# x + ctx of a fused attention and low-rank-expert block made by ScalarE and GpSimd at the head of a pass, the first w in contiguous halves, one wait of the second sample left out

## The reference

```
p = Wp @ layernorm(x);  t = Wt @ ctx;  g = Wg @ ctx
att[group] = sum over the group's 32 rows of p * g
y = Wz(grouped) @ (att * t)
w = x + tanh(g_xattn) * (groupnorm(y) * gn_w + gn_b + ctx)
h = layernorm(w, axis=-1)
gate = softmax over the 16 largest of h @ Wq.T @ keys.T, spread over 64 experts
z = (h @ A.T) * gate (each expert has 8 columns)
out = w + tanh(g_ffn) * 2 * (z @ B.T)
```

## Time and profile before

| what | us |
|---|---|
| median of 3 runs | 340.39 (338.96 to 341.20) |
| the profiled execution's own time | 341.37 |
| its span | 339.6 |
| PE busy | 331.7 (98% of the span) |
| DVE busy | 246.2 (73%) |
| ACT busy | 161.6 (48%) |
| POOL busy | 162.5 (48%) |

### The profile page before, as it was taken

One profiled execution on the slowest core, in us unless ns is written; L12 is line 12 of the kernel. 1 busy time (PEld: TensorE's weight loads), 2 busy tenths in 40 slices (PEclk: granted clock), 3 DMA queues, 4 the chain that ended last, 5 costly groups with the idle time before them and its releaser, 6 DMA issues.

```text
span 339.6 us, 5620 instructions
## 1 busy us (share of the span) xinstructions
PE 331.7 (98%) x2024; PEld 298.8 (88%) x2024; DVE 246.2 (73%) x625; ACT 161.6 (48%) x286; POOL 162.5 (48%) x146
## 2 busy tenths in 40 slices
PE   8999999999999999899999999999999999999996
PEld 6588898899988998788999899898999899989984
DVE  0866996684779879678797697867897785773462
ACT  2596835684374453375516662183535632342310
POOL 0173798199158599055940859036860620010000
PEclk9998999999999999799999999999999999999999
DMA  7999702960912574159521874238621121103002
GB/s 252 409 388 398 279 2 55 353 212 5 322 46 93 182 284 124 31 162 299 194 72 26 245 280 154 62 108 296 234 77 33 32 92 41 54 3 124 2 31 93
DMA packets 21227, 52.21 MB, mean 154 GB/s; under 512 B 2112, under 2 KB 6848, under 8 KB 21200
## 3 DMA queue, kind: packets, MB, share of 16 engines
q1 hardware_dynamic: 20848, 51.65, 44.2%
q10 hardware_dynamic: 352, 0.20, 0.2%
HBM read 41.10 MB, written 10.75 MB: 153 GB/s over the span
## 4 chain that ended last, share of the span: by engine, by line
PE 85%; DVE 8%; POOL 4%; issue 2%; DVEq 0%; POOLq 0%
PE w_ps L1205 16%; PE z_ps L1175 16%; PE w_ps L1091 10%; PE w_ps L1175 9%; PE w_ps L1212 8%; PE z_ps L1042 7%; PE z_ps L1021 4%; PE t_ps L1152 3%; PE w_ps L1069 2%; PE w_ps L1042 2%; PE t_ps L1119 2%; POOL c_lo L365 1%; DVE x_st L706 1%; POOL A_lo L353 1%; PE w_ps L1219 1%
## 5 line engine op out<-in xcount | busy, mean ns | idle before, releaser
L1205 PE MATMUL w_ps<-B_hi,zT_hi 128*128 128x512 f32 x128 | 51.9, 406 | 0.0
L1205 PE MATMUL w_ps<-B_lo,zT_hi 128*128 128x512 f32 x128 | 50.2, 392 | 0.0
L346 POOL TENSOR_TENSOR xT_lo<-xT_in,xT_hi 128x512 fp32r<-128x512 f32 x24 | 35.5, 1498 | 22.0 <-ACT xT_hi L458 19.2
L389 POOL TENSOR_TENSOR y_rs<-y_ve,minus_half 128x2 f32<-128x2 f32 x8 | 5.9, 742 | 71.4 <-DVE y_ve L789 71.4
L365 POOL TENSOR_TENSOR c_lo<-c_sb,c_hi 128x512 fp32r<-128x512 f32 x24 | 30.3, 1303 | 11.7 <-DVE uw L811 11.7
L346 POOL TENSOR_TENSOR cT_lo<-cT_in,cT_hi 128x512 fp32r<-128x512 f32 x24 | 35.5, 1500 | 0.0
L1175 PE MATMUL z_ps<-A_hi,hT_hi 128*128 128x288 f32 x160 | 34.7, 298 | 0.3 <-POOL A_lo L353 0.3
L1212 PE MATMUL w_ps<-B_hi,zT_lo 128*128 128x512 f32 x128 | 34.5, 391 | 0.0
L508 ACT ACTIVATE uw<-w_ps,neg_u 128x512 f32<-128x512 f32 x32 | 20.1, 684 | 30.2 <-DVE neg_u L756 30.2
L1175 PE MATMUL z_ps<-A_lo,hT_hi 128*128 128x288 f32 x160 | 34.1, 295 | 0.0
L525 ACT ACTIVATE hT_hi<-t_ps 128x512 fp32r<-128x512 f32 x32 | 17.5, 595 | 27.9 <-PE t_ps L1152 27.3
(11 more groups left out here) (164 smaller groups left out, 860.7 us busy)
## 6 DMA issues: line engine op xcount, KB each, us to landing
c_sb<-in_ctx SPq DMA_DIRECT2D x16, 512.0 KB, 5.5
x_sb<-in_x SPq DMA_DIRECT2D x16, 512.0 KB, 5.2
xT_in<-in_xT SPq DMA_DIRECT2D x14, 512.0 KB, 7.8
cT_in<-in_cT SPq DMA_DIRECT2D x14, 512.0 KB, 9.1
out_block<-uw SPq DMA_DIRECT2D x14, 512.0 KB, 4.3
z_through<-zg_sb SPq DMA_DIRECT2D x9, 256.0 KB, 2.3
products<-z_through SPq DMA_DIRECT2D x9, 256.0 KB, 2.7
A_in<-in_aT SPq DMA_DIRECT2D x8, 256.0 KB, 12.4
```

Source lines behind the costliest of these rows:

```text
L346: last = pool.tensor_tensor(lo[:, chunks, :], came[:, chunks, :], hi[:, chunks, :].bitcast(f32), ALU.subtract)
L1205: pe.matmul(w_ps[k][:, :], zT_hi[:, t, row], w[:, j, cols], start=(j == 0 and w is B_hi), stop=False)
```

## The change

Four things are edited.

1. From sample 3 on, x + ctx is made by `scale_ctx` on ACT and `x_add` on POOL. `scale_ctx(3)` stands behind `hT_high(1, 2)`, and `scale_ctx(m + 1)` at the end of ACT's pass, behind `hT_high(1, m)`. `x_add(m)` is the first thing in POOL's pass. `x_shift` on POOL and `x_plus_ctx` on DVE are gone from sample 3 on and stay for sample 2. ACT's `exps(0, b)` now stands between the two halves of the transposes' high parts.
2. In DVE's pass `zT_low(0, b)` stands between the two tiles of w, and `minus_means(m + 1)` (which makes beta) behind `zT_low(1, b)`, where it stood ahead of `zT_turn(1, b)`.
3. `first_w(k)` works on contiguous halves of a tile and waits for that quarter's copy of u alone; `hT` of sample 0 waits for `w_done` in both of its groups.
4. `group_means(2)` doesn't wait for `att_rows`.

```
--- before.py
+++ after.py
@@ -374,7 +374,8 @@
 
             def x_add(n):
                 for t in range(T):
-                    pool.wait_ge(c_scaled, per_tile(n, t))
+
+                    pool.wait_ge(c_scaled, per_tile(n if n < 2 else n - 1, t))
                     for cols in pieces():
                         last = pool.tensor_tensor(c_sb[n % 2][:, t, cols], c_sb[n % 2][:, t, cols], x_sb[:, t, cols],
                                                   ALU.add)
@@ -430,8 +431,8 @@
             x_root(3)
             w_root(2)
             c_low(3)
-            x_shift(3)
             for m in range(3, NB):
+                x_add(m)
                 if m + 1 < NB:
                     for h in range(NH):
                         xT_low(h, m + 1)
@@ -443,8 +444,6 @@
                     pool.wait_ge(w_done, per_tile(m, T - 1))
                     c_low(m + 1)
                 w_root(m)
-                if m + 1 < NB:
-                    x_shift(m + 1)
 
         @block.scalar
         def _(act):
@@ -615,11 +614,6 @@
             w_square(1)
             hT_high(1, 1)
             offsets(1)
-            def transposes_high(n):
-                for h in range(NH):
-                    xT_high(h, n)
-                    cT_high(h, n)
-
             for t in range(T):
                 c_high(t, 2)
             residual(1)
@@ -643,11 +637,16 @@
             offsets(2)
             M_high(3)
             hT_high(1, 2)
+            scale_ctx(3)
             for b in range(2, NB - 1):
                 m = b + 1
                 if m + 1 < NB:
-                    transposes_high(m + 1)
+                    xT_high(0, m + 1)
+                    cT_high(0, m + 1)
                 exps(0, b)
+                if m + 1 < NB:
+                    xT_high(1, m + 1)
+                    cT_high(1, m + 1)
                 residual(b)
                 if b < NB - 2:
                     exps(1, b)
@@ -669,6 +668,8 @@
                     M_high(m + 1)
                 hT_high(0, m)
                 hT_high(1, m)
+                if m + 1 < NB:
+                    scale_ctx(m + 1)
             residual(NB - 1)
             exps(0, NB - 1)
             zT_high(0, NB - 1)
@@ -696,7 +697,7 @@
 
                 dve.wait_ge(c_lo_s, from_second(n, T - 1))
                 for t in range(T):
-                    dve.wait_ge(x_shifted, per_tile(n - 2, t))
+                    dve.wait_ge(x_shifted, t + 1)
                     dve.scalar_tensor_tensor(c_sb[n % 2][:, t, :], c_sb[n % 2][:, t, :], tg[:, 0:1], x_sb[:, t, :],
                                              ALU.mult, ALU.add).then_inc(xt_done, 1)
 
@@ -797,15 +798,15 @@
 
             def first_w(k):
 
-                t, g = divmod(k, NH)
-                rows, sums = (parts(a[0][:, t, :])[:, g * KH:(g + 1) * KH, :] for a in (uw, c_sb))
-                dve.wait_ge(u_copied, per_use(0, NH * t + NH - 1))
+                t, cols = use(k)
+                dve.wait_ge(u_copied, per_use(0, k))
                 dve.wait_ge(xt_done, per_tile(0, t))
-                dve.scalar_tensor_tensor(rows, rows, slope[:, t:t + 1], sums, ALU.mult, ALU.add).then_inc(
-                                             w_done if k % NH == NH - 1 else w_half, 1)
-
-            def w_tiles(n):
-                for t in range(T):
+                last = dve.scalar_tensor_tensor(uw[0][:, t, cols], uw[0][:, t, cols], slope[:, t:t + 1],
+                                                c_sb[0][:, t, cols], ALU.mult, ALU.add)
+                last.then_inc(w_done if k % NH == NH - 1 else w_half, 1)
+
+            def w_tiles(n, tiles=range(T)):
+                for t in tiles:
                     dve.wait_ge(u_copied, u_use(n, NH * t + NH - 1))
                     dve.wait_ge(xt_done, per_tile(n, t))
                     dve.scalar_tensor_tensor(uw[n % 2][:, t, :], uw[n % 2][:, t, :], slope[:, t:t + 1],
@@ -963,7 +964,6 @@
             minus_means(3)
             for b in range(2, NB - 1):
                 m = b + 1
-                x_plus_ctx(m)
                 gate(0, b)
                 if b < NB - 2:
                     x_stats(m + 1)
@@ -973,12 +973,13 @@
                 u_statistics(m, (0,))
                 group_deviation(m)
                 slopes(m, lambda: zT_turn(0, b))
-                w_tiles(m)
+                w_tiles(m, (0,))
                 zT_low(0, b)
+                w_tiles(m, (1,))
                 if b < NB - 2:
-                    minus_means(m + 1)
                     zT_turn(1, b)
                     zT_low(1, b)
+                    minus_means(m + 1)
                     gram_fix(m + 1)
                     M_low(m + 1)
                     add_out(0, b)
@@ -1124,7 +1125,7 @@
             def group_means(n):
                 pe.wait_ge(u_stats, per_tile(n, T - 1))
                 pe.wait_ge(cb_s, n + 1)
-                if n >= 2:
+                if n >= 3:
                     pe.wait_ge(att_rows, per_tile(n, T - 1))
                 pe.matmul(t_ps[1][:, 0:T], group_mean[:, :], u_mv[:, :, 0], start=True,
                           stop=True).then_inc(mean_sum, 1)
@@ -1137,10 +1138,7 @@
 
             def hT(t, n):
                 for g in range(2):
-                    if n == 0 and g == 0:
-                        pe.wait_ge(w_half, t + 1)
-                    else:
-                        pe.wait_ge(w_done, per_tile(n, t))
+                    pe.wait_ge(w_done, per_tile(n, t))
                     if t > 0:
                         pe.wait_ge(hT_lo_s, per_use(n, g))
                     elif g == 0 and n > 0:
```

## The result

The changed kernel takes 344.31 us (median of 4 runs, 343.60 to 345.89); beside it the kernel before took 339.74 (338.96 to 341.20). The ratio is 1.013, with a 95% interval of 1.009 to 1.017. The forecast was 341.9, with a range up to 344.0, that is, 1.5 us more than before; it became 4.6 us more. The sign of the sum was right, its size was not. The profiled execution took 344.0, its span is 342.2.

What follows compares the result with a forecast made beforehand. PE, busy 98%, bounds the kernel, so only its waits count. -0.6 at b = 2 (swallowing the earlier -0.8 and -0.75) and +2.1 after it gave +1.5: 341.9 us on the median, range 336.0 to 344.0.

Steps and rivals of the forecast that it cites:

- First w: First w and POOL's first lots: contiguous quarters let the lots start 0.9 earlier; gain 0.8 us, bounds 0 and 1.0.
- `group_means(2)`: PE's wait for att_rows goes: 0.6 us plus 0.15 for overlap, together 0.75; bounds 0 and 0.8.
- b = 2: Pass b = 2: late x and held L713, L714; zg_done 0.6 earlier, slow matmuls stay; 0.5 lost to 4.3 gained.
- The steady passes: Passes b = 3 to 5: POOL holds L713, L714; new PE wait of 0.7 us each, 2.1 together.
- Rival 1: L713 and L714 not held, no steady wait: 337.9, or 336.1 if the clock stays up; chance 0.27 (0.17 clock kept).
- Rival 2: Clock falls in the new 0.7 us waits, second half of u_product, 1.8 each in three passes: 347.3; chance 0.07.
- Rival 3: The gate itself is held by POOL, 0.65 more in each of three steady passes: 343.9; chance 0.04.
- The reordered ends: Moved zT_low(0, b), minus_means and w's tile 1 at pass ends: counted 0, bounds -0.1 and +0.1 a pass.

Runs made afterwards that it cites:

- run 3: The changed kernel with x + ctx from sample 3 on again by POOL and DVE, no scale_ctx there, all else kept: 339.13 us, ratio 1.000.
- run 6: The kernel of run 3 with the two tensor_scalar of x_moments split into one element a row: 336.07 us, ratio 0.989.
- run 11: The changed kernel a second time, unaltered, for its profile: 344.68 us in one run.
- run 8: The changed kernel with POOL's x_add and low parts in pieces of 128x256 instead of 512 columns: 361.07 us, ratio 1.062.
- run 2: The changed kernel with the two 128x2 tensor_scalar of x_moments split into four of 128x1, in their old place: 337.20 us, ratio 0.993.
- run 1: The changed kernel with x_moments(m + 1) moved from ahead of gate(1, b) to behind att_reduce(m): 335.56 us, ratio 0.990.
- run 5: The kernel before with only the two tensor_scalar of x_moments split into one element a row: 338.12 us, ratio 0.996.
- Run 7: As run 2, with x_moments and b = 2's last bn_stats behind zT_turn(1, b), and x_root(m + 1) behind y_root(m): 334.77 us, ratio 0.986.
- run 4: The kernel before with four more POOL tensor_tensor over 128x512 into an unused tile, ahead of the low parts: 339.93 us, ratio 1.000.
- run 10: The changed kernel with each half's low part in samples 4 and 5 as one POOL instruction on 128x1024: 347.54 us in one run.
- run 9: The changed kernel with POOL waiting for its own last instruction between any two of the eight low parts: 340.28 us, ratio 0.999.

## Why the prediction was wrong in size and right in kind

- **First w, and `group_means(2)`: right.** Three quarters take 2.08 us (forecast 1.95), POOL's three lots start at 34.45 instead of 36.40 (0.85 of it by the change, the rest by the start; forecast 0.9), the waits of the earlier trace rows are gone. By the passes the gains are 0.80 and 0.69 (forecast 0.8 and 0.75). In the changed kernel 1.05 of them went into a longer wait at b = 2, as the text had it; in the profile of run 3, with x + ctx on DVE, they reach the restart at b = 2 in full (1.4), and in run 6, with the holds away, the median shows them too.
- **b = 2: right.** The load of x ends the wait before the last bn_stats, L714 and L715 reach one POOL end each (0.75 and 1.34), the restart is 0.45 earlier by the change (forecast 0.6), and the clock still falls. The slow matmuls got 0.3 shorter, which the forecast didn't have.
- **The steady passes: right in place, wrong in size. This is the step that failed:** "So L713 is held to 174.05, L714 to 175.3 ... a new wait of 0.7 us, in each of three passes, 2.1 together. For each the bounds are 0 and 1.35 (one or two whole POOL steps, less the cover)." The passes became 0.7, 2.0 and 2.0 longer in one profile (4.7) and 2.0 each in the other (6.0). All times that lead up to this were right: counted from z_product, L714 starts at 12.54 (forecast 12.5) and POOL's stream ends at 15.73 in b = 3 (forecast 15.8). What failed is the length of the hold. Behind it stood the rule "each of the two can be held to the end of a POOL instruction", taken from the earlier trace rows. The trace of before has a second such case, at 48.5 us, where the two take 0.61 and 1.31 (so two L714 in eight were long, not one); both cases were released at the next end, and neither shows that an end can be missed. In the profile of after and in run 11 the first of the two is held past two ends, in run 8 past seven and eight. The upper bound should have been the end of POOL's stream: 176.6 by the forecast's own numbers, less 175.3, is 1.3 more a pass, 2.0 in place of 0.7. Had the bound been worked out so, the range would have reached 341.9 + 3 x 1.3 = 345.8.
- **Rival 1 (not held) is out** in the changed kernel; run 2 (337.2, with the clock up at b = 2 beside a wait of 1.2) is what it would have been, between the two times given for it (337.9 and 336.1). **Rival 2 (the clock falls in the new waits) is out** in the changed kernel: idle times of 0.49 and 1.81 us left it at 1.00. In run 8 it fell beside waits of 3.5 and 7.1. **Rival 3 (the gate itself is held) is out:** from L842 to the end of L867 the gate takes 3.14 in b = 4, where POOL is busy for 0.7 of it (214.24 to 217.38), and 3.15 at b = 2, where POOL is busy all through (132.38 to 135.53). But I had taken the rule of the Trainium skill (SBUF — State Buffer, SBUF: two separate sides) too widely there. The gate has one tensor_scalar from SBUF to SBUF, `neg_max`, and it is 128x1 (0.15 us at b = 2); by the condition of the Trainium skill quoted at run 2 it can't run in the two-port mode, so that it doesn't take the shared port. The gate's length speaks for the Trainium skill, not against it. Read in full, the Trainium skill names the two held instructions in advance.
- **The reordered ends: at the good end of the bounds.** Forecast were 0, and -0.1 to +0.1 a pass. Where nothing is held, a steady pass takes 38.85 with them (runs 1, 2 and 6) and 38.94 to 38.97 without (run 5): 0.1 a pass gained, 0.3 in all. Run 7, with `x_moments` put between these ends, is back at 38.94. Which of the reorderings does it isn't shown.

What stays open is why one end of a POOL instruction releases DVE and another doesn't. All holds seen fall in two kinds, to the first end or to the end of the stream, and none to an end between; but the same program at the same point fell in either (run 11 and the profile of after). No run here separates the cause.

## What to carry to other kernels

When work moves to GpSimd, look in VectorE's stream for short operations on SBUF with an even number of elements a row, and for what stands behind them: two of them, 0.16 us each, took this kernel up to 3.3 us a pass in front of a gate that TensorE waited for. Bound such a hold by the end of GpSimd's unbroken stream, not of its next instruction. And ask whether the work taken off an engine stood ahead of anything the critical engine waits for: here, with the holds gone, moving x + ctx left the steady passes as they were. Cures by size: shape them as one element a row (7 us here, with nothing else touched), put them behind the operation that the critical engine waits for (9 us), or leave a gap of 0.1 us between GpSimd's instructions (4 us); cutting GpSimd's work in smaller pieces, without gaps, made it worse (17 us).

## What the runs showed of the hardware that was not expected

- A VectorE tensor_scalar over 128x2 from SBUF to SBUF was held for 3.22 us (two POOL ends missed, in the profile of after and in run 11) and 4.90 and 5.52 us (seven and eight, run 8); over 128x1 none was: the 16 that make `x_ve` in run 2 took 0.14 to 0.15 us each, those beside a busy POOL among them.
- Ends were missed only where POOL's stream ran without a gap, and not always there (runs 4 and 10); with gaps of some 0.1 us all eight operations of run 9's four passes were free or released at the next end.
- The length of PE's wait alone doesn't account for the granted clock. It stayed at 1.00 beside waits of 1.81 us in the steady passes and of 1.2 and 1.1 at b = 2 (runs 2 and 4), and fell to 0.50 beside 1.88, 1.90, 2.2 and 2.9 at b = 2 (before, runs 3 and 9, after); but it also fell to 0.50 at 24 to 28 us in the profile of before, where PE has no idle time.
- That early fall came in some executions and not in others of programs that are the same up to there (runs 9 and 10 have it, after and run 11 don't), and costs 1.6 us. Two profiles are better compared from a point behind such a place, pass by pass.
